# A two-layer transformer block on one core: where the second attention's maxima, context copies and first loads are done

## The reference, cut to what matters

```
Q = x @ wq + bq; K = x @ wk + bk; V = x @ wv + bv
Q = Q.reshape(B * H, S, D); K = ...; V = ...       # H = 16, D = 16, S = 1024
scores = einsum('bqd,bkd->bqk', Q, K) / sqrt(D)
attn = softmax(scores, axis=-1)
ctx = einsum('bqk,bkd->bqd', attn, V).reshape(B, S, E)
out = ctx @ wo + bo + x                              # then a layer norm
```

## Time and profile before

| | us |
|---|---|
| median of 3 runs | 2868.09 (2867.3 to 2884.91) |
| the profiled execution | 2862.78 |
| its span | 2861.1 |
| projection stage, begin to end | about 1545 to 1706 |
| attention stage | about 1706 to 2553 |

### The profile page before, as it was taken

The page is one execution under the profiler, slowest core; times in us unless marked ns, Lnnn a source line. Parts: engine busy times, 40 slices in busy tenths (PEclk is TensorE's granted clock), DMA queues, the critical chain, the costliest instruction groups (busy, mean ns, idle before and its releaser), DMA issues. The chain is left out here.

```text
span 2861.1 us, 45814 instructions
## 1 busy us (share of the span) xinstructions
PE 2298.1 (80%) x15498; PEld 1384.6 (48%) x15499; DVE 1683.0 (59%) x2646; ACT 997.4 (35%) x1893; POOL 423.3 (15%) x559
## 2 busy tenths in 40 slices
PE   3988888686989999999796838889898888955233
PEld 2666666475855555555685723333333333315122
DVE  4667677544433333333464428888888888828763
ACT  2444444212310000000222304667676766732001
POOL 3000000014400000000243300000000000011016
PEclk9999999858999999999898967999999999975557
DMA  6000000045721111111333799335554442021016
GB/s 206 2 0 0 0 0 0 10 167 177 257 78 35 35 35 35 34 36 31 121 120 107 267 143 86 26 30 42 49 42 41 43 39 18 1 63 59 0 60 205
DMA packets 217555, 193.00 MB, mean 67 GB/s; under 512 B 116394, under 2 KB 193362, under 8 KB 215410
## 3 DMA queue, kind: packets, MB, share of 16 engines
q1 hardware_dynamic: 198386, 140.07, 25.7%
q0 software_dynamic: 16768, 34.90, 4.1%
q10 hardware_dynamic: 2304, 16.78, 1.6%
HBM read 109.62 MB, written 81.79 MB: 67 GB/s over the span
## 5 line engine op out<-in xcount | busy, mean ns | idle before, releaser
L1622 DVE TENSOR_REDUCE ga_nmax<-banks 128x1 f32<-128x1024 f32 x512 | 611.4, 1221 | 167.6 <-PE banks L1683 166.6
L1656 ACT ACTIVATE ga_probT<-banks 128x512 f32<-128x512 f32 x1024 | 542.6, 600 | 278.2 <-PE banks L1696 278.1
L1683 PE MATMUL banks<-a_ks,a_qs 48*128 48x512 f32 x1024 | 359.9, 456 | 112.8 <-DVE ga_nmax L1622 65.3
L1696 PE MATMUL banks<-a_qs,a_ks 49*128 49x512 f32 x1024 | 386.6, 459 | 6.9 <-ACT ga_probT L1656 3.6
L1683 PEld LDWEIGHTS banks<-a_ks,a_qs 48*128 48x128 f32 x1024 | 159.3, 192 | 385.7 <-DVE ga_nmax L1622 258.2
L1183 PE MATMUL banks<-m_w,rb_xT 128*128 x576 | 288.9, 624 | 0.0
L1711 PE MATMUL banks<-ga_probT,a_v 128*32 128x512 f32 x2048 | 276.0, 612 | 14.9 <-ACT ga_o L1662 14.9
L1165 ACT ACTIVATE rb_silu<-banks 128x512 f32<-128x512 f32 x72 | 43.0, 597 | 516.7 <-PE banks L1183 516.7
L1030 PE MATMUL banks<-sh_xnT,sh_w 128*128 128x512 f32 x768 | 182.9, 397 | 18.6 <-DVE sh_w L943 9.6
L1696 PEld LDWEIGHTS banks<-a_qs,a_ks 49*128 49x128 f32 x1024 | 162.4, 186 | 71.9 <-ACT ga_probT L1656 67.5
L1610 POOL DMA_DIRECT2D a_qs<-ga_max_rows x128 | 64.2, 508 | 735.2 <-DVE ga_max_rows L1627 735.2
(11 more groups left out here) (291 smaller groups left out, 3510.7 us busy)
## 6 DMA issues: line engine op xcount, KB each, us to landing
sh_xnT<-xnT_parts ACTq DMA_DIRECT2D x16, 1024.0 KB, 5.7
sorted_rows<-wa_zero SPq DMA_DIRECT2D x1, 9216.0 KB, 29.1
rb_xb<-sorted_rows POOLq DMA_DIRECT2D x72, 128.0 KB, 2.3
sorted_out<-rb_yb SPq DMA_DIRECT2D x72, 128.0 KB, 1.7
xnT_parts<-np_parts SPq DMA_DIRECT2D x8, 1024.0 KB, 4.5
m_w<-in_L_ffn_rw_dram SPq DMA_DIRECT2D x2, 4096.0 KB, 25.7
values<-pg_v SPq DMA_DIRECT2D x16, 512.0 KB, 2.7
a_qs<-queries_rounded SPq DMA_DIRECT2D x32, 256.0 KB, 8.5
```

What stands on the lines that cost most here:

```text
L1622: nc.vector.tensor_reduce(nmax[arg // UB % 2][:, at:at + 1], slot[:], axis=AX.X, op=ALU.max, negate=True).then_inc(use_read, 1)
L1656: nc.scalar.activation(probT[k % SETS][2 * h + n][:], b_t[w % RING][:], ACT.Exp, scale=SCALE).then_inc(exp_ready, 1)
L1683: return nc.tensor.matmul(slot[:, HALF * kh:HALF * (kh + 1)], qs[a][rows, n, P * q:P * (q + 1)], ks[a][rows, n, HALF * kh:HALF * (kh + 1)] ...
L1696: nc.tensor.matmul(b_t[w % RING][:], ks[a][rows, 2 * gp + n, P * kt:P * (kt + 1)], qs[a][rows, 2 * gp + n, HALF * hf:HALF * (hf + 1)], sta ...
```

## The change

In the projection stage the 14 loads of super 0 move from behind iteration 6 to behind iteration 1; the iterations 2 to 6 follow them on SP. In the attention stage: the maxima no longer use a slot. After a block's last reduction DVE waits for its own result and transposes the 128 x 32 tile of maxima in 32 x 32 blocks, SBUF to SBUF; SP, not POOL, places the rows, with 16 DMAs a block (one for each of four 32-row pieces, two n and two h) in place of four. SP issues all 14 loads of super 1 first, then block by block the maxima and behind them a quarter of a later super's loads. `context` moves from step 5 to step 6 of its 16, behind `weigh`. ACT's `outputs` moves from behind the exponentials of step 3 to behind those of step 4. The copies of `contextT` move from DVE to ACT, behind the exponentials of the step after it.

```
@@ project_groups, SP
             keep_x(0)
-            with sp.Fori(0, STEPS - 1) as r:
+            for r in range(2):
                 keep(r, 0)
                 keep_x(r + 1)
                 keep(r, 1)
...
                 load_values(sp, 0, h, v[0], values, first_in)
+            with sp.Fori(2, STEPS - 1) as r:
+                keep(r, 0)
+                keep_x(r + 1)
+                keep(r, 1)
             for s in range(2):
                 keep(STEPS - 1, s)
@@ group_attention, step_uses
-        if s % UB == 1 and UB < s < UNITS + UB:
-            uses.append(("maxima", s // UB - 1))
         b, j = (s - LAG) // UB - 1, (s - LAG) % UB
-        if 0 <= b < BLOCKS and j == 5:
+        if 0 <= b < BLOCKS and j == 6:
             uses.append(("context", b))
@@ SP
+            def maxima(b):
+                c, gp, hf = block_of(b)
+                q_cols = qs[c % SLOTS][:, :, HALF * hf:HALF * (hf + 1)].bitcast(F32)
+                sp.wait_ge(rows_ready, ONE + b + 1)
+                for h in range(2):
+                    at = HR * h + ST
+                    for n in range(2):
+                        dst = q_cols[at:at + 1, 2 * gp + n].rearrange("o (q j p) -> o q j p", q=HQ, p=BL)
+                        for j in range(P // BL):
+                            first = BL * j + UB // 2 * h + HQ * n
+                            sp.dma_start(dst[:, :, j, :], max_rows[b % 2][first:first + HQ].bitcast(F32)).then_inc(max_in[b % 2], 16)
+
+            for h in range(2):
+                for n in range(2):
+                    load(1, h, n)
+            for b in range(BLOCKS):
+                maxima(b)
+                c, gp, hf = block_of(b if b < 4 else b - 2)
+                if (b < 4 or b >= 6) and c + 2 < SUPERS:
+                    load(c + 2, gp, hf)
@@ DVE
+                        if arg % UB == UB - 1:
+                            if b >= 2:
+                                dve.wait_ge(max_in[b % 2], ONE + MAX_IN * (b // 2))
+                            dve.wait_ge(use_read, ONE + read_count[use])
+                            nc.vector.transpose(max_rows[b % 2][:].bitcast(F32), nmax[b % 2][:].bitcast(F32)).then_inc(rows_ready, 1)
@@ ACT
+            def context_copy(m):
+                use = use_place["contextT", m]
+                act.wait_ge(use_done, ONE + use + 1)
+                for h in range(2):
+                    src = b_s[use % 2][:, 2 * P * h:2 * P * (h + 1)].rearrange("p (n a t) -> p n a t", a=A, t=GT)
+                    nc.scalar.activation(ctxT[:, h].rearrange("p a n t -> p n a t"), src, ACT.Copy).then_inc(ctxT_ready, 1)
+
             for back in range(UNITS):
                 for n in range(2):
                     weights(back, n)
-                if back % UB == 3 and back > UB:
+                if back % UB == 4 and back > UB:
                     outputs(back // UB - 1)
+                if back % (2 * UB) == 9 and back > UB:
+                    context_copy(back // (2 * UB) - 1)
             outputs(BLOCKS - 1)
+            context_copy(BLOCKS // 2 - 1)
@@ PE
             def slot_of(use):
                 if use >= 2:
-                    pe.wait_ge(use_read, ONE + use - 1)
+                    kind, arg = uses[use - 2]
+                    if kind == "contextT":
+                        pe.wait_ge(ctxT_ready, ONE + 2 * (arg + 1))
+                    else:
+                        pe.wait_ge(use_read, ONE + read_count[use - 2])
                 return b_s[use % 2]
...
-            def maxima(b):
-                slot = slot_of(use_place["maxima", b])
-                pe.wait_ge(use_read, ONE + use_place["scores", UB * (b + 1) - 1] + 1)
-                nc.tensor.transpose(slot[:, 0:P], nmax[b % 2][:], g.ident[:]).then_inc(use_done, 1)
```

More of the change, by code:

```diff
@@ L106, in setup @@
     g.ident = sb("ident", [P, P])
-    g.unused = [c.enter_context(nc.semaphore(f"pool_dma{n}")) for n in range(24)]
+    g.unused = [c.enter_context(nc.semaphore(f"pool_dma{n}")) for n in range(22)]
     g.bank2 = [c.enter_context(nc.psum_tensor(f"banks{i}", [P, 1024], F32)) for i in range(4)]
@@ L1526, in group_attention @@
     RING = 3
+    MAX_IN = 16 * 4 * P // BL
     RB = UB // 2
@@ L1554, in step_uses @@
         return uses
-    use_place = {use: n for n, use in enumerate(use for s in range(STEPS) for use in step_uses(s))}
+    uses = [use for s in range(STEPS) for use in step_uses(s)]
+    use_place = {use: n for n, use in enumerate(uses)}
+    read_count = [sum(kind != "contextT" for kind, _ in uses[:n + 1]) for n in range(len(uses))]
     with phase(nc) as (e, semaphore, begin):
@@ L1563, in group_attention @@
         o = [sb(f"o{s}", [P, HALF]) for s in range(2)]
-        nmax = [sb(f"nmax{s}", [P, P]) for s in range(2)]
-        max_rows = [sb(f"max_rows{s}", [UB, P], F32R) for s in range(2)]
+        nmax = [sb(f"nmax{s}", [P, BL], F32R) for s in range(2)]
+        max_rows = [sb(f"max_rows{s}", [P, BL], F32R) for s in range(2)]
         rsum = [sb(f"rsum{s}", [P, HQ, NG]) for s in range(2)]
@@ L1570, in group_attention @@
         qk_in, v_in = [sem(f"qk_in{a}") for a in range(SLOTS)], [sem(f"v_in{a}") for a in range(SLOTS)]
-        max_in = g.pool_dma(2)
+        max_in = [sem(f"max_in{s}") for s in range(2)]
         use_done, use_read, sT_done, exp_ready, pv_done, o_ready = [sem(n) for n in (
             "use_done", "use_read", "sT_done", "exp_ready", "pv_done", "o_ready")]
-        rsum_ready, stats_ready = sem("rsum_ready"), sem("stats_ready")
+        rsum_ready, stats_ready, ctxT_ready, maxima_ready, rows_ready = [sem(n) for n in (
+            "rsum_ready", "stats_ready", "ctxT_ready", "maxima_ready", "rows_ready")]
         b_s, b_t, b_o = g.bank2[0:2], g.bank[4:4 + RING], g.bank[7]
@@ L1582, in _, with load @@
                 sp.dma_start(wo[q * DH:(q + 1) * DH], wo_rows[q]).then_inc(w_in, 16)
-            for c in range(1, SUPERS):
+            def maxima(b):
[9 more added lines that the diff above has]
+                            sp.dma_start(dst[:, :, j, :], max_rows[b % 2][first:first + HQ].bitcast(F32)).then_inc(max_in[b % 2], 16)
+            def load(c, h, n):
                 a = c % SLOTS
-                if c >= SLOTS:
+                if c >= SLOTS and h == n == 0:
                     sp.wait_ge(sT_done, ONE + 8 * UB * (c - SLOTS + 1))
                     sp.wait_ge(pv_done, ONE + 4 * RB * (c - SLOTS + 1))
[L1588 to L1593, removed]
-                    load_values(sp, c, h, v[a], values, v_in[a])
+                load_part(sp, c, h, n, (qs[a], ks[a])[n], parts, qk_in[a])
+                if n == 1:
+                    load_values(sp, c, h, v[a], values, v_in[a])
+            for h in range(2):
[6 more added lines that the diff above has]
+                    load(c + 2, gp, hf)
         @block.gpsimd
@@ L1598, in _ @@
             for s in range(2):
[L1599 to L1610, removed]
+                nc.gpsimd.memset(nmax[s][:].bitcast(F32), 0.0).then_inc(nmax_zero, 1)
         @block.vector
@@ L1635, in _ @@
                                                 rsum[hf][:].unsqueeze(3).broadcast_to([P, HQ, NG, DH]), ALU.mult).then_inc(use_read, 1)
[L1636 to L1641, removed]
+                    elif kind == "project":
                         c, gp, h = block_of(arg)
@@ L1735, in project @@
                 slot = slot_of(use_place["project", b])
-                pe.wait_ge(use_read, ONE + use_place["contextT", b // 2] + 1)
+                pe.wait_ge(ctxT_ready, ONE + 2 * (b // 2 + 1))
                 if b == 0:
@@ L1743, in project @@
                 last.then_inc(use_done, 1)
-            other = {"maxima": maxima, "context": context, "contextT": context_T, "project": project}
+            other = {"context": context, "contextT": context_T, "project": project}
             for s in range(STEPS):
@@ L1759, in _ @@
                     scores_T(back, 1)
-                if back >= 4 and back % 2 == 0 and back <= UNITS + 2:
+                if 4 <= back <= UNITS + 2 and back % 2 == 0:
                     weigh(back // 2 - 2)
```

16 lines of the change are left out of this document (7 added, 9 removed).

## The result

| | before | after |
|---|---|---|
| median of 5 runs (us) | 2868.09 (2862.83 to 2884.91) | 2916.91 (2899.11 to 2918.89) |
| the profiled execution; its span | 2862.78; 2861.1 | 2899.11; 2897.5 |
| ratio of the times | | 1.0149, 95% interval [1.0106, 1.0192] |

The changed kernel is 1.5% slower. The median is 25 us above the 2892 that was forecast, and 1 us above the upper end of the range. The profiled execution was the shortest of the five, 36 above its counterpart before, against the 24 of the sum.

The account below looks back on a forecast made before the run. The prediction took the plain loop as bound by a chain through PE, the first exponential and `weigh` (2.61 us a pair). First loads -4, steady part +14 and ramp +14 gave +24 on 2868.09, so 2892 us, range 2855 to 2916.

Parts of the forecast that it names:

- rival that ACT's new order is hidden: Attention stage: `weigh` and step 10 do not feel ACT, so +30 and +22 go, 2840 us; chance 0.10.
- Outputs, +30: Steps 3 and 4: `weigh` waits for the later output copy, +0.98 us in each of 31 blocks.
- Copies on ACT, +22: Steps 9 and 10: step 10's scores wait for ACT's `contextT` copies, 1.54 us above plain, 14 times.
- Maxima off PE, transposes, context: -33 + 9 - 14 = -38: Attention blocks: mid-pair use gone, -33 us; scores wait behind DVE's transpose, +9; `context` behind `weigh`, -14.
- three uses of 1.1: Attention loop before: three slot uses between a pair's two steps were said to cost 1.1 us each.
- Ramp, +14: Attention start: block 0's maxima land behind super 1's 14 loads, at 1758; PE, DVE and ACT stand still, +14 us.
- SP too slow (the rival): Attention blocks: 16 DMAs a block do not fit from 0.65 us an issue; at 0.8, +38, 2930 us; chance 0.12.
- First loads early, -4: Projection stage: early loads stall stores and PE by about 33 us mid-stage in place of the end; gain 4 us.

Follow-up runs that it names:

- e2_out3: The changed kernel with only the output copy back behind step 3's exponentials; 2869.72 us, ratio 1.0003 to before.
- e11_before_out4_fill: The kernel before with outputs behind step 4 and four repeated score matmuls in the wait ahead of `weigh`; 3005.14 us, ratio 1.0163.
- e9_spread: The changed kernel with outputs behind step 3, `contextT` copies on DVE, super 1's and 2's loads spread between blocks' maxima; 2915.77 us against 2966.83, ratio 0.9851.
- e1: The changed kernel again with no edit; 2912.99 us against 2868.74 for the kernel before, ratio 1.0157.
- e3: The changed kernel with four repeats of a step 4 score matmul on PE in the wait for outputs; 2902.54 us, ratio 1.0126 to before.
- e4: The changed kernel with only the copies of `contextT` back on DVE; 2900.54 us, ratio 1.0117 to before.
- e6: The changed kernel with super 0's loads back behind iteration 6; 3009.68 us against 2966.97 for the kernel before, ratio 1.0163.
- e12: The changed kernel with `contextT` copies back on DVE and four repeated score matmuls in the wait for outputs; 2878.92 us against 2871.49 before, ratio 1.0037.
- e10_before_out4b: The kernel before with only the output copy moved from behind step 3 to behind step 4; 3123.2 us against 2966.83.

## Why the prediction was right, and where it was not

- **Direction and mechanism: right.** Slower, by the two ACT moves, against the maxima's gain. The forecast's rival that ACT's new order is hidden fell: the outputs' wait is 1.46, and e2_out3 gives 43 us back.
- **Outputs, +30: right as a wait.** Forecast 3.15 from pair start to `weigh`, measured 2005.79 - 2002.64 = 3.15; e11_before_out4_fill's body is 31 over before's.
- **Copies on ACT, +22: a little too high.** Forecast a pair of 4.15, measured 3.88, so +18. The two copies take 0.67 together, not the 0.84 taken from twice the 469 ns of the earlier trace rows.
- **Maxima off PE, transposes, context: -33 + 9 - 14 = -38.** The -33 cannot be read from a pair, since the use is gone; context with the transpose measured -7, so -40, and e9_spread's body, with these edits and neither ACT move, is 38 below before's. The transpose takes 0.21 (forecast 0.20), and the scores behind `context` wait 0.19 for DVE. The prediction's "three uses of 1.1" are two, `context` and `maxima`; the sum does not depend on it.
- **Ramp, +14.** Measured +10 in the first profile, with 48.2 from the stage's start against the 51 to 54 of the forecast; six others with this order of SP (e1, e2, e3, e4, e6, e12) have 49.6 to 54.8. The step holds, though by another sum: SP took 0.63 for an issue, not 0.42 (a length; begin to begin the `wo` loads of the earlier trace rows take 3.95 / 8 = 0.49), and the loads ahead ended sooner (the first small DMA was issued at 1735.56, not at about 1747).
- **SP too slow (the rival): half right.** An issue is 0.63, near the 0.65 from which it would decide; 16 of them are 10 us in each block, and no block behind the first waits. So it stays off the path, just.
- **First loads early, -4.** The gap on PE is there, 33.25 for the 33 worked out, and ended at 1631.50 for about 1630. The sum -4 against the -6.8 of the profiles cannot be told from nothing, since the stage's length varies by 8 to 10 us from profile to profile.
- **The step that failed: the sum itself, by a term that was not in it.** With the waits as measured it gives -7 + 10 + 8 = +11. The body holds 16 more, and the tail 9, and nearly all of these 25 is what 0.36 of the added time at 0.50 comes to (16 and 8). The prediction reckoned with the clock's lower level only where PE starts again in the projection stage, and had no term for it in the attention stage, where before ran at 1.00. In e12_ctxdve_fill a kernel with one of the two waits gets 23 back when only the clock is mended, and in e2_out3 13 of the 43 us are more than the wait.
- **Luck.** In the profiled executions the whole is 36 for the 24 of the sum. The terms that were in it came out 13 too high together (copies 4, ramp 4, first loads 3, maxima and context 2), which hid half of the missing 25. The median, 2916.91, is 25 above the forecast and 1 above the range. That this is 25 too is chance: the profiled execution was the shortest of the five.
- **Open.** The two waits' shares do not add up: 30 is left over with only the outputs late (103.5 us at 0.50), 14 with only the copies (44.0), 13 to 16 with both (46.5 and 53.5). Why both together are no worse than the one is not shown.

## What to carry over

When an edit puts a wait of some 1.5 us (here 1.46 and 1.50) into TensorE's stream in every turn of a busy loop, price the wait and then ask for the clock: read PEclk in windows before and after, and look for matmuls of nearly double length behind the wait. An engine that copies a result which the very next TensorE group needs must do it first, ahead of other work that has slack. In a queue that issues in order, spread bulk loads between the small urgent transfers; putting them ahead of, or all behind, the first urgent one only chooses which block pays.

## What the hardware showed that was not expected

- Behind waits of 1.46 to 1.50 us on PE the granted clock fell to 0.50 for 3.4 to 17 us at a time, though not behind every such wait. The waits of 0.48 and 1.05 of the kernel before brought no fall in its body. But the length of a wait is not the whole of it: at eight places in e3_fill, e11_before_out4_fill and e12_ctxdve_fill the clock fell at a wait of 0.76, behind the repeated matmuls. Where the waits of `context` and `maxima` stand in the next two pairs, the windows fell to 0.77 (e10_before_out4b). The Trainium skill, TensorE: Matmul & The Clock Gate, section "A second HAM failure mode: psum-queue depth-cycling", tells of a kernel that swings between the two levels because PE idles briefly between groups of matmuls; these rows agree.
- Useless matmuls in a wait can be worth about 100 us (e11_before_out4_fill's body against e10_before_out4b's): five of its six windows are at 1.00 and one at 0.98.
- The fall need not come at once: at 2028.34 the eight matmuls behind the wait still took 1.07, and the granted clock fell at about 2030.2, 1.8 us later.
- One of SP's maxima DMAs, four runs of 128 bytes, costs SP 0.57 us to issue and 0.63 from one to the next, where a `wo` load costs 0.42 and 0.49.
